# A fused attention and mixture-of-experts block: routed images in five groups instead of six, and the unrouted image wholly behind the last block

## What is computed

```
x = x + rmsnorm(W_out @ linear_attention(W_qkv @ rmsnorm(layernorm(x))) + b_out) * g_out   # per image, 4 heads of 32
t = tokens of x
p = softmax(layernorm(t) @ gate_w + gate_b)             # 8 experts
keep the two largest of p per token (not renormalised)
t = t + sum over the two kept experts e of p_e * (gelu(layernorm(t) @ W1[e] + b1[e]) @ W2[e] + b2[e])   # 128 -> 256 -> 128
```

## Time and profile before

| | |
|---|---|
| median of 3 runs | 755.87 us (751.54 to 756.84) |
| the profiled execution | 758.1 us |
| its span in the trace | 756.4 us |
| mean granted TensorE clock | 0.94 |
| instructions | 15759 |
| PE busy | 658.9 us (87%) |
| DVE busy | 562.6 us (74%) |
| ACT busy | 535.5 us (71%) |
| POOL busy | 481.0 us (64%) |
| DMA | 159.28 MB, mean 211 GB/s |

### The profile page before, as it was taken

One profiled execution on the slowest core, in us unless ns is written; L12 is line 12 of the kernel. 1 busy time (PEld: TensorE's weight loads), 2 busy tenths in 40 slices (PEclk: granted clock), 3 DMA queues, 4 the chain that ended last, 5 costly groups with the idle time before them and its releaser, 6 DMA issues. The chain is left out here.

```text
span 756.4 us, 15759 instructions
## 1 busy us (share of the span) xinstructions
PE 658.9 (87%) x4074; PEld 545.3 (72%) x4074; DVE 562.6 (74%) x2178; ACT 535.5 (71%) x1388; POOL 481.0 (64%) x504
## 2 busy tenths in 40 slices
PE   3867689889899798999879989998899899998995
PEld 2553478768588577977758867876789788887884
DVE  5889879999899987999778889788679522332342
ACT  2643348787787597879869778686698765676764
POOL 1002635717777677777767777777777775777773
PEclk9987779999999899999989999999699999999997
DMA  7801358458777776896667978884799899659622
GB/s 176 227 19 39 129 183 251 139 175 262 228 201 233 226 230 189 250 271 208 224 218 228 277 224 233 238 262 147 218 282 308 280 294 345 203 149 288 205 78 84
DMA packets 110208, 159.28 MB, mean 211 GB/s; under 512 B 19216, under 2 KB 74536, under 8 KB 110120
## 3 DMA queue, kind: packets, MB, share of 16 engines
q1 hardware_dynamic: 93704, 126.58, 54.7%
q0 software_dynamic: 15360, 31.49, 13.9%
q10 hardware_dynamic: 1056, 0.22, 0.2%
HBM read 103.81 MB, written 57.02 MB: 213 GB/s over the span
## 5 line engine op out<-in xcount | busy, mean ns | idle before, releaser
L840 POOL DMA_INDIRECT rows_in<-xf_tok,row_of x240 | 242.8, 1012 | 179.3 <-DVE row_of L1401 90.9
L855 POOL DMA_INDIRECT y_rows<-rows_out,row_back x240 | 235.8, 982 | 84.6 <-issue 76.5
L1640 PE MATMUL y_ps<-wb,hid 128*128 128x128 f32 x1552 | 207.2, 283 | 17.2 <-ACT hid L957 15.9
L1640 PEld LDWEIGHTS y_ps<-wb,hid 128*128 128x128 f32 x1552 | 189.5, 194 | 36.4 <-ACT hid L957 33.3
L957 ACT ACTIVATE hid<-h_ps,wb 128x256 f32<-128x256 f32 x388 | 162.2, 474 | 55.7 <-PE h_ps L1630 53.1
L1630 PE MATMUL h_ps<-xt,wb 128*128 128x256 f32 x648 | 171.3, 389 | 7.0 <-DMA wb<-experts 5.8
L1630 PEld LDWEIGHTS h_ps<-xt,wb 128*128 128x128 f32 x648 | 114.8, 196 | 21.2 <-DMA wb<-experts 6.9
L1468 DVE TENSOR_TENSOR yb<-y_ps,wb 128x256 f32<-128x256 f32 x162 | 68.0, 420 | 81.2 <-PE y_ps L1640 80.0
L1550 PE MATMUL ab<-wqkv_t,x_sb 128*128 128x392 f32 x256 | 107.8, 556 | 11.9 <-ACT xt L951 4.8
L943 ACT ACTIVATE y_rows<-y_rows,share 128x128 f32<-128x128 f32 x240 | 80.9, 406 | 34.1 <-DMA y_rows<-rows_out,row_back 33.7
L895 ACT ACTIVATE qkv<-ab,root 128x392 f32<-128x392 f32 x128 | 72.4, 589 | 32.7 <-PE ab L1550 26.1
(11 more groups left out here) (195 smaller groups left out, 970.0 us busy)
## 6 DMA issues: line engine op xcount, KB each, us to landing
wb<-experts SPq DMA_DIRECT2D x162, 321.0 KB
xb<-rows_in SPq DMA_DIRECT2D x162, 128.0 KB
rows_out<-yb SPq DMA_DIRECT2D x162, 128.0 KB
rows_in<-zeros SPq DMA_DIRECT2D x69, 128.0 KB, 2.8
x_sb<-in_x_dram SPq DMA_DIRECT2D x16, 512.0 KB, 4.4
out_dram<-out_sb SPq DMA_DIRECT2D x32, 256.0 KB, 3.0
rows_in<-xf_tok,row_of POOLq DMA_INDIRECT x240
y_rows<-rows_out,row_back POOLq DMA_INDIRECT x240
```

Source lines behind the costliest of these rows:

```text
L840: pool.indirect_dma_start(out=rows_in[p % IN_BUFS], out_offset=bass.IndirectOffsetOnAxis(ap=row_of[:, n % X1_RING, k, t:t + 1], axis=0), i ...
L855: pool.indirect_dma_start(out=y_rows[:, r, k, :], out_offset=None, in_=rows_out[p % OUT_BUFS][0:BLOCKS[p] * ROWS, :], in_offset=bass.Indir ...
L1640: last = pe.matmul(y_ps[:, b % Y_BUFS, i * P:(i + 1) * P], hid[:, b % 2, k, i * P:(i + 1) * P], wb[:, r, HIDDEN + k * CH:HIDDEN + (k + 1) ...
```

## The change

The routed images go in groups of 1, 3, 4, 4 and 3 instead of 1, 2, 3, 4, 4 and 1. So there are five plans instead of six, and 15 + 31 + 39 + 39 + 31 = 155 blocks instead of 15 + 23 + 31 + 39 + 39 + 15 = 162. All 32 chunks of image 15 stand behind the last block; before, 16 stood ahead of the last group's blocks and 16 behind. `x_sb` has three places instead of two; to make room, `cw_t` (image 15's expert weights, transposed) lies in the buffer `square`, which is free by then. A send's first half waits for the first half of the normed tokens only. Three steps get one more ordering edge in the planner's list. All bonuses are other numbers.

```diff
-GROUPS = (1, 2, 3, 4, 4, 1)
+GROUPS = (1, 3, 4, 4, 3)
...
-X_RING, TOK_RING, QKV_RING, PAIR_RING = 2, 3, 2, 3
+X_RING, TOK_RING, QKV_RING, PAIR_RING = 3, 3, 2, 3
...
-    "middle": (18.5, 36.9, 0.0, 22.1, 22.4, 16.1, -44.7, 107.2, 6.0, 114.2, 13.0, -135.7, 0.6, 10.5, -48.1, -14.8),
+    "middle": (-2.1, -5.0, 39.1, 10.3, 1.4, 1.8, -30.7, -1.6, 31.1, 2.5, 17.5, 57.8, -9.0, -50.8, 52.3, -33.8),
...
-DENSE_AHEAD = {0: (0, 0, 0, 23, 23, 34, 46, 46), BATCH - 1: (ALL_BLOCKS - BLOCKS[-1],) * 4 + (ALL_BLOCKS,) * 4}
+DENSE_AHEAD = {15: (ALL_BLOCKS,) * 8}
...
-        step("ACT", a("x_tok0"), 0.48, [a("X0")] + old("x1_1", TOK_RING), 0.2, table="any")
+        step("ACT", a("x_tok0"), 0.48, [a("X0")] + chain("x_tok1") + old("x1_1", TOK_RING), 0.2, table="any")
...
-        step("DVE", a("k_shift"), 1.14, [a("KB")], 0.1)
+        step("DVE", a("k_shift"), 1.14, [a("KB")] + chain("k_shift"), 0.1)
...
-            step("POOL", of("send", n, t), 2.49, [a("place"), a("xf1")] + before + ([("turn", BLOCK0[p - IN_BUFS + 1] - 1)] if p >= IN_BUFS else []), 3.0)
+            step("POOL", of("send", n, t), 2.49, [a("place"), a("xf0" if t < HT else "xf1")] + before + ([("turn", BLOCK0[p - IN_BUFS + 1] - 1)] if p >= IN_BUFS else []), 3.0)
...
-        cw_t = sb("cw_t", [EXPERTS, TOK])
+        cw_t = square[0:EXPERTS, :, :].rearrange("p t c -> p (t c)")
...
-        s_x_in = [sem("x_in0"), sem("x_in1")]
+        s_x_in = [sem(f"x_in{r}") for r in range(X_RING)]
...
+                if t % HT == 0:
+                    pool.wait_ge(s_xf, n * 2 + 1 + t // HT)
                 if t == 0:
-                    pool.wait_ge(s_xf, n * 2 + 2)
                     pool.wait_ge(s_place, PLACE * (m + 1))
```

More of the change, by code:

```diff
@@ new lines @@
+    "back": (-70.5, 61.0, -76.3, 0.0, 24.9, 220.1, 46.1, -29.4, 0.0, 51.7, 4.2, -56.1, 8.4, -16.4, -12.9, 0.0),
+    "begin": (0.8,),
+    "block": (7.8, -59.0, -8.1, -121.0, -103.5),
+    "dense": (16.2, 0.0, -98.2, 8.4, 0.5, 69.9, -14.7, 3.2),
+    "early": (-69.7, -29.9, -13.0, 0.0, 142.4, 294.4, 6.1, 0.0, 41.6, -55.6, 140.8, 125.5, 0.0, 8.7, -2.8, -11.1),
+    "fetch": (30.4, 36.9, -112.1, 23.7, -76.4, -64.6, -49.1, -2.7, -92.2, 2.9, -3.3, 20.1, 34.4, 59.2, 0.0, 0.0),
+    "join": (54.4, 132.1, 48.0, 8.8, -18.0, 3.6, -19.5, 0.0, -1.1, -1.5, 83.0, -148.4, 15.6, -15.8, -67.3, 16.5),
@@ L71 @@
+    "late": (-167.4, -4.1, 1.3, 1.8, 147.9, 23.8, 0.0, -0.0, -0.6, 10.1, -13.1, -4.0, 29.7, 133.0, 112.4, 0.1),
+    "send": (0.0, 3.2, -33.7, 54.3, 3.9, -1.2, 146.1, 16.9, 5.7, -52.8, -88.4, -32.9, -120.9, 45.4, -34.9, 0.0),
+    "table": (-53.3, 8.6, 24.9, 8.6, -19.0),
 }
 FAVOURED_KIND = {
[3 rows of a table removed]
-    "bn1_0": 30.3, "bn1_1": 251.8, "bn2_1": 39.8, "center": -6.4, "choose": 4.3, "copy_w": -15.6, "ctx": 76.4, "ctx_t": -1.2,
-    "cw_t0": -18.0, "cw_t1": 1.2, "down": -61.6, "exp_k": -7.6, "exp_q": -5.1, "experts": 0.8, "fetch": 11.3, "first": -216.4,
@@ L78 @@
-    "fold_gate": -3.3, "fold_out": -10.5, "fold_w": -113.0, "gelu": 5.4, "gx": -4.4, "ident": 2.0, "inverse": -90.3, "k_max": 433.2,
-    "k_part": -10.1, "k_shift": 345.1, "load": 17.1, "load_w": 75.4, "load_x": -9.3, "logits": -58.8, "logits0": -26.6, "mix": -11.0,
[4 rows of a table removed]
-    "turn": -8.8, "turn_g": 17.9, "turn_s": -15.0, "turn_w": -38.6, "up": -145.2, "weigh": -176.7, "wload": 292.1, "x1_0": -19.5,
-    "x1_1": -16.6, "x_ch0": -2.7, "x_ch1": 22.3, "x_tok0": -9.9, "x_tok1": -45.9, "xf0": -169.0, "xf1": -4.2, "xt": 198.8,
@@ L86 @@
-    "zero": 3.5,
[4 rows of a table added]
+    "ctx": -101.5, "ctx_t": 13.7, "cw_t0": 1.1, "cw_t1": -85.8, "down": 7.2, "exp": 1.2, "exp_k": -3.9, "exp_q": 25.8,
+    "experts": 4.0, "fetch": -1.0, "first": 4.9, "fold_gate": 9.3, "fold_w": 20.1, "gelu": -3.0, "gx": 15.2, "ident": 15.5,
+    "inverse": -25.0, "k_max": -98.6, "k_part": 13.5, "k_shift": -12.1, "load": -83.3, "load_w": -24.4, "load_x": 23.7, "logits": -123.4,
[4 rows of a table added]
+    "store": 3.4, "store_out": 16.2, "table": -3.7, "take": 0.9, "turn": 69.6, "turn_g": -1.8, "turn_s": -111.1, "turn_w": -24.8,
@@ L87 @@
+    "up": -0.5, "weigh": -0.6, "wload": -22.5, "x1_0": 3.0, "x1_1": -154.0, "x_ch0": 21.8, "x_ch1": 8.6, "x_tok0": 3.7,
+    "x_tok1": -27.9, "xf0": -12.3, "xf1": -1.7, "xt": 58.8, "zero": 74.8,
 }
@@ L195, in attention @@
         step("PE", a("M"), 0.24, [a("ctx_t"), ("fold_out", 0)], 0.25, "M", [a("mix")])
-        step("DVE", a("mix"), 0.22, [a("M")] + old("F2", 2), 0.1)
+        step("DVE", a("mix"), 0.22, [a("M")] + chain("mix") + old("F2", 2), 0.1)
         for h, size in enumerate((0.71, 0.71, 0.48)):
@@ L205, in attention @@
         for h in range(2):
-            step("DVE", a(f"x1_{h}"), 0.6, [a(f"norm{h + 1}")] + ([a("x1_0")] if h else []), 0.1)
+            step("DVE", a(f"x1_{h}"), 0.6, [a(f"norm{h + 1}")] + ([a("x1_0")] if h else chain("x1_1")), 0.1)
             parts("DVE", a(f"bn2_{h}"), (0.39, 0.39), [a(f"x1_{h}")] + ([a("bn2_0")] if h else chain("stats2")), 0.1)
```

10 lines of the change are left out of this document (removed), and 15 rows, old and new, of the table FAVOURED_KIND.

## The result

| | before | changed |
|---|---|---|
| median | 753.70 us (749.62 to 756.84, 4 runs) | 773.10 us (769.99 to 777.41, 4 runs) |
| ratio | | 1.0242, 95% interval 1.0199 to 1.0284 |
| the profiled execution | 758.1 us | 777.4 us |
| its span | 756.4 us | 775.4 us |
| mean granted TensorE clock | 0.94 | 0.915 |

The change made the kernel 2.4% slower. The forecast was 753 us, in a range of 738 to 766. One execution of experiment 1 (792.57 us, at a granted clock of 0.815 against 0.921 to 0.933 in its others) was in a slower state and is left out of the ratios.

The account below looks back on a forecast made before the run. POOL's DMA queue was taken as the bound: image 6's send at 262 us, 480.7 us of DMAs behind it and a 10.7 us tail give a 753.4 us span; forecast 753 us from the median, range 738 to 766.

Parts of the forecast that it names:

- Net 8.4 us of DVE's work, 9 us at 91% busy: ready at 269.5 - 9 = 260.5: DVE's list ahead of image 6's row numbers: loses 12.7 us of work, gains 4.3, so they are ready at 260.5 us.
- the forecast 262: POOL's queue: image 6's send was to start at 262 us, with 368 DMAs behind its start.
- The second term: End of the kernel, from POOL's last fetch through weighing, adds, transposes, copy and store: 10.7 us, as before.
- The budget of POOL's queue: POOL's DMAs, the gaps between them and real waits, with lead and tail, account for the whole 756.4 us span before.
- a wait of 23.9 us at image 6: POOL ahead of image 6's send: forecast to wait 15 to 20 us for row numbers, replacing waits at images 1 and 3.
- By itself that costs nothing: POOL's first send: moving from 69.9 to about 95 us was to cost no time by itself.
- The last group's fetch: POOL near the end: the 6.9 us wait ahead of this fetch falls away, with 12 us of cover.
- its own term: PE's end: 73 us of blocks, 63 of chunks, about 10 of output transposes, done at 739 to 742 us.
- The 5 us: Last group, transfer after its first load: an estimate of 5 us more, giving 593 us.
- Rival 1: DVE reaches image 6 10 to 16 us sooner by closing half its idle time: 743 us (738 to 748), chance 0.22.
- Rival 2: PE is the bound, so the seven blocks' 16.5 us of PE work come off: 739 us, chance 0.08.
- Rival 3: DVE held by a block without rows, so POOL waits again for images 12 to 14: 765 us (760 to 772), chance 0.22.

Follow-up runs that it names:

- experiment 1: Changed kernel with image 6's choice, exponential, count and row numbers ahead of image 8's gate step: 774.47 us, ratio 1.0263 to the kernel before.
- experiment 2: Changed kernel with the weighting of image 0's last tile moved behind image 8's q, k, v copies on ScalarE: 766.96 us, ratio 1.0150 to the kernel before.
- experiment 7: Changed kernel with image 0's last weighting later, image 15's outputs ahead of image 14's, and 86 added TensorE transposes (images 0, 1): 757.34 us, ratio 1.0015.
- experiment 9: Changed kernel with image 0's last weighting later, image 15's outputs ahead of image 14's, and 252 added TensorE transposes (images 0 to 3): 750.80 us, ratio 0.9932.
- experiment 10: Kernel before with 150 unread transposes added on TensorE at steps of images 0 to 3: 747.28 us, ratio 0.9873.
- experiment 11: Changed kernel with the 252 added TensorE transposes alone, both orders left as they were: 764.56 us, ratio 1.0147 to the kernel before.
- experiment 12: Kernel before with image 15's two output halves behind image 14's, nothing else changed: 761.13 us, ratio 1.0090.
- experiment 5: Changed kernel with image 0's last weighting later on ScalarE and image 15's outputs ahead of image 14's: 759.17 us, ratio 1.0026 to the kernel before.
- experiment 3: Changed kernel with image 0's choice, count and row numbers earlier, so the first send starts sooner: 775.55 us, ratio 1.0291 to the kernel before.
- experiment 4: Kernel before with one added wait: POOL's first send waits for image 1's row numbers: 774.04 us, ratio 1.0241.
- experiment 6: Changed kernel without the second expert's row fetches for images 13 and 14, 16 POOL DMAs fewer: 768.03 us, ratio 1.0134 to the kernel before.

## Why the prediction was wrong

**The step that failed** is "Net 8.4 us of DVE's work, 9 us at 91% busy: ready at 269.5 - 9 = 260.5". Row numbers came at 279.0. The work ahead of them was counted by kinds of instruction, and the idle time was carried over as a share. VectorE (the third of the busy times) up to image 6's row numbers, in the kernel before:

```profile
0.00:269.30 269.30, 218.31 (x1228) 169.05 (x1229) 235.40 (x1012) 169.38 (x424) 124.17 (x145) 0.90 0.61 179
```

and in the changed one:

```profile
0.00:279.00 279.00, 210.91 (x1159) 167.06 (x1160) 232.82 (x973) 166.49 (x412) 117.30 (x136) 0.86 0.53 158
```

Its busy time fell by 2.6 us instead of 8.4, and its idle time rose from 269.3 - 235.4 = 33.9 to 279.0 - 232.8 = 46.2 us, by 12.3. Carried over as a share it would have fallen.

The count itself was right. Seven takes, a plan, two adds and the rest are gone, and the durations of all of VectorE's instructions up to there add up to 302.0 us before and 294.2 after, 7.8 less. But consecutive instructions overlap in time, and in the new order they do so by 5.2 us less. What in the order does that is not shown.

Idle time is a list of waits, and the new list has other ones. Two are named and tested. One is image 8's gate step, held by the weighting of image 0's last tile (experiment 2: 7.8 us at image 6's send). The other is the low clock while attention runs alone (experiments 7 and 9: 7.7 us more, from 272.9 to 265.2). Together they bring the send within 3 us of the forecast 262. But the second also exists in the kernel before, from whose rows the forecast started. There the transposes gave 2.7 us at image 6's row numbers and 5.2 at image 3's send (experiment 10), so only 2.5 to 5 of the 7.7 us count against the change. Some 5 to 8 of the 18 us are then left without a cause shown. The lost overlap of 5.2 us may be most of that; no run tests it. Nor do the two causes simply add up: in experiment 11 the transposes alone brought the send to 263.1.

**The second term** that failed is the tail, carried over as 10.7 us. It measured 16.1. Experiment 12 makes the same of the old kernel by the order of two images' outputs alone (16.1 us in its profiled execution, ratio 1.0090), and experiment 5 takes it away. I had looked at what moved near POOL and VectorE, and not at what the new block count does to a sort key at the end.

**What held.** The budget of POOL's queue as the frame of the sum: 368 DMAs at 1.302 us (1.306 in the sum), the first send at 94.4 (90 to 97), a wait of 23.9 us at image 6 (15 or more), no wait over 1.1 us behind it. "By itself that costs nothing", of the first send: right for this list (experiment 3), and experiment 4 shows that it isn't a rule, since in the other list a delay of 24 us costs 19. (The waits in the budget add up to 54.1 us where 53.5 stands; nothing rests on the difference.) The last group's fetch had no wait, as said. PE's last chunk ended at 755.6 us, just ahead of POOL's last fetch, but its own term was short: PE's busy time fell by 8.3 us and not by the 16.5 of the seven blocks, and from the last group's first load (604.0) to the last chunk it took 151.6 us where 5 + 73 + 63 = 141 were reckoned. The 5 us, an estimate without a row, came out at 4.9 (from that load to the group's first transpose at 608.95). In part the longer time is the clock (0.92 behind 583 us, where it had been 0.96).

**The rivals.** Rival 1 (VectorE sooner) had the sign wrong: the lists' idle time grew. Rival 2, PE as the bound, had a page of the Trainium skill for it (Perfetto Trace Analysis, Identifying the Most-Contended Engine). But the same section judges TensorE's headroom by MFU (the share of its peak rate) and by its weight loads, and not by matmul busy time. The weight loads were busy for 72%, less than VectorE's 74%. In the profiles 8.3 us fewer of PE's busy time went with 19 more of span, so the highest occupancy did not name the bound here. Yet experiment 6 shows that TensorE's and ScalarE's lists would end the kernel only some 9 us sooner than POOL's. Experiment 9 adds 17.6 us to PE's busy time (636.6 in experiment 5, 654.3) and gains 7. Rival 3 had the right sign but the wrong place. Behind image 6's send POOL never waited for more than 1.1 us. My chance of 0.19 for a slower kernel was too low above all since each of my sums took what wasn't counted (idle time, tail, clock) to stay as it was.

**The groups themselves** were not changed alone in any run, so their price is not shown. With the weighting and the outputs in another order the changed kernel comes to 1.0026 (1.0002 to 1.0051); with TensorE kept busy, to 0.9932 where the kernel before comes to 0.9873. These are different edits at different places, so the 0.6% between them is no price of the groups, but it shows no gain. That the seven fewer blocks don't pay fits what was found: they are not in POOL's list. The third place for input images, `cw_t` in `square`, the half wait, the ordering edges (four, since `mix` and `x1_0` get one too, and not three) and the new bonuses were not tried alone.

## What to carry to other kernels

Where a planner makes the lists, cost a change by the waits in the new lists: take every cross-engine dependence on the path to the deciding send, ask what each waited-for engine has ahead of it in its own list, and look for circles (here a fetch, its weighting, a copy, a product, a gate step, and again the send). A share of idle time must not be carried over. Look at the last ten instructions of every engine, since a sort key that depends on a count can turn round. And where an engine with a clock gate has gaps on the path to the first transfers, cheap work in its gaps may be worth as much as the order of the lists. Here it took 1.3% off the kernel before, which no new order alone did; the two orders of experiment 5 gave the changed kernel 2.2% back.
